# Adjacency network, eight graphs on one core: twenty-four step tiles ahead of the second widening, three guard products in front of the second aggregation, the older normalisation beside the first one

## What is computed

```
x = layernorm(x + attention(x, adj))       # softmax(q k^T * scale, masked by adj) v
x = layernorm(x + leaky(norm_adj @ x @ W.T + b))
x = layernorm(x + heads(x, adj))           # 4 heads: softmax over i of leaky(s_i + s_j), masked; times Wh
x = layernorm(x + (D^-1/2 (adj + I) D^-1/2) @ x @ B)
```

## Time and profile before

| what | us |
|---|---|
| median of 3 runs (lowest to highest) | 1005.48 (1004.79 to 1006.26) |
| the profiled execution | 1003.88 |
| its span, first to last instruction | 1002.0 |
| busy in the span: PE, DVE, ACT, POOL | 860.9, 744.5, 588.7, 334.8 |
| idle of DVE ahead of head minima (L825, both buffers), for ACT's step tiles | 77.2 |
| idle of DVE ahead of layer 3's output, for PE | 37.4 |
| mean granted clock of TensorE | 0.937 of full speed |

### The profile page before, as it was taken

How to read it: one execution, slowest core, us unless ns; L and a number is a source line. 1 busy time by engine, 2 the same in 40 slices (tenths; PEclk the granted TensorE clock), 3 DMA queues, 4 the chain that set the end, 5 groups by cost and what they waited for, 6 DMA issues and landing times.

```text
span 1002.0 us, 25308 instructions
## 1 busy us (share of the span) xinstructions
PE 860.9 (86%) x10852; PEld 689.5 (69%) x10852; DVE 744.5 (74%) x1635; ACT 588.7 (59%) x667; POOL 334.8 (33%) x335
## 2 busy tenths in 40 slices
PE   4985899879999799888998799987998979985774
PEld 3663589747887479855797468964788747973773
DVE  4325775968778695977959788695959779597986
ACT  1672485566764578465764667655685557735432
POOL 2021250416324152243504253240622425134504
PEclk9997899979999999998999999997999999998788
DMA  9701415450356414480174503554044721505100
GB/s 186 114 22 31 97 53 97 86 127 1 85 87 133 80 43 94 66 166 18 43 128 86 128 1 85 87 120 92 17 100 61 165 42 43 106 3 127 43 25 21
DMA packets 166607, 77.91 MB, mean 78 GB/s; under 512 B 136640, under 2 KB 154176, under 8 KB 166496
## 3 DMA queue, kind: packets, MB, share of 16 engines
q1 hardware_dynamic: 157008, 59.00, 28.7%
q0 software_dynamic: 8448, 16.78, 9.4%
q10 hardware_dynamic: 1040, 0.52, 0.2%
HBM read 55.18 MB, written 4.33 MB: 59 GB/s over the span
## 4 chain that ended last, share of the span: by engine, by line
PE 62%; DVE 25%; issue 5%; ACT 4%; POOL 0%; DVEq 0%; POOLq 0%; ACTq 0%
PE ring L1267 12%; PE Z L1282 11%; PE ring L1213 10%; PE ring L1248 9%; PE Z L1235 8%; DVE cmat L825 6%; DVE x L861 3%; PE ring L1211 2%; DVE ring L770 2%; DVE rest L944 2%; PE ring L1176 2%; ACT maskb L608 2%; PE ring L1181 1%; DVE meanvar L854 1%; DVE small L912 1%
## 5 line engine op out<-in xcount | busy, mean ns | idle before, releaser
L660 ACT ACTIVATE steps<-sjrow,steepsi 128x1024 bf16<-128x1024 f32 x248 | 267.3, 1139 | 96.1 <-DVE cmat L825 85.8
L1267 PE MATMUL ring<-vparts,cmat 128*128 128x66 bf16 x4416 | 161.2, 200 | 44.2 <-DVE cmat L825 28.3
L1267 PEld LDWEIGHTS ring<-vparts,cmat 128*128 128x128 f16 x4416 | 154.8, 102 | 50.8 <-DVE cmat L825 32.5
L825 DVE TENSOR_TENSOR cmat<-steps,adj 128x1024 f16<-128x1024 bf16 x180 | 152.0, 893 | 13.0 <-ACT steps L660 11.0
L1213 PE MATMUL ring<-qT,xT 128*128 128x512 f32 x256 | 151.7, 677 | 0.0
L488 POOL TENSOR_SCALAR vareps<-meanvar 128x4 f32<-128x4 f32 x64 | 16.6, 260 | 391.0 <-DVE meanvar L854 391.0
L1235 PEld LDWEIGHTS Z<-vv,probs 128*128 128x128 f32 x1024 | 123.0, 192 | 35.1 <-issue 21.7
L624 ACT ACTIVATE wide<-adjT 128x1024 fp32r<-128x1024 f16 x128 | 124.7, 1045 | 37.5 <-PE Z L1282 37.5
L1235 PE MATMUL Z<-vv,probs 128*128 128x129 f32 x1024 | 125.5, 276 | 13.1 <-ACT probs L667 9.0
L1282 PE MATMUL Z<-wide,parts 128*128 128x512 f32 x512 | 128.1, 402 | 9.6 <-DVE parts L870 5.1
L667 ACT ACTIVATE probs<-ring 128x1024 f32<-128x1024 f32 x64 | 65.3, 1020 | 118.7 <-PE ring L1213 118.7
(11 more groups left out here) (118 smaller groups left out, 1217.4 us busy)
## 6 DMA issues: line engine op xcount, KB each, us to landing
adj<-in_adj_dram POOLq DMA_DIRECT2D x16, 1024.0 KB, 12.8
sjrow<-sj_rows SPq DMA_DIRECT2D x32, 512.0 KB, 4.2
out_dram<-x SPq DMA_DIRECT2D x16, 256.0 KB, 2.4
x<-in_x_dram SPq DMA_DIRECT2D x7, 512.0 KB, 5.5
adjT<-adj SPq DMA_TRANSPOSE x128, 3.4
x<-in_x_dram ACTq DMA_DIRECT2D x1, 512.0 KB, 4.2
small<-in_a_dram SPq DMA_DIRECT2D x1, 128.0 KB, 10.3
sj_rows<-steps SPq DMA_DIRECT2D x8, 16.0 KB
```

Source lines behind the costliest of these rows:

```text
L660: act.activation(steps[:, n % STEPS, :], sjrow[:, h % 2, :], ACT.Relu, bias=steepsi[:, t, h:h + 1], scale=STEEP).then_inc(step_made, 1)
L825: dve.tensor_tensor(c_of[:, t, :], steps[:, n % STEPS, :], adjs[o.parity][:, t, :], ALU.min)\
L1267: last = pe.matmul(s[:, jt, 0:VW], c_of[:, t, jt * P:(jt + 1) * P], vparts[:, t, h, part, :], start=t == 0 and part == 0, stop=t == T - 1 ...
```

## The change

Five orders are changed; no instruction is added or taken out. (1) ACT makes 24 instead of 20 step tiles ahead of the second half of the first widening. (2) In a full step, the guard products 0 to 2 of the following graph run on PE ahead of `agg3` and product 3 between the two outputs of `agg3` (before: only product 0, there; 1 to 3 at the start of the next step). With them, ACT makes mask tiles 0, 1, 2 right after it has taken `xT`, `q` and `v`, and tile 3 after `agg3`; and DVE casts x and q and reads `wh` ahead of `split_x3`, and makes guards 0 to 3 ahead of layer 3's outputs. (3) The statistics and the application of the older graph's last normalisation move on DVE from the context loop to the first aggregation; POOL's 1/sqrt for it and SP's store follow. (4) Head 2's minima are made in one go, and head 3's directly after head 0's combination, ahead of layer 1's outputs; the mask sums are read after head 2's minima. (5) `groups_of` follows the new order of products.

```diff
@@ groups_of
-        if n < 2:
-            seq += of(n, ("s", 0))
-        seq += of(n, *[("s", t) for t in range(1, 5)])
+        seq += of(n, *[("s", t) for t in range(0 if n < 2 else 4, 5)])
...
-        seq += of(n - 1, ("out3", 0))
-        if n > 0:
-            seq += of(n + 1, ("s", 0))
-        return seq + of(n - 1, ("out3", 1))
+        early = n > 0
+        seq += of(n + 1, *[("s", t) for t in range(3) if early]) + of(n - 1, ("out3", 0))
+        return seq + of(n + 1, *[("s", t) for t in (3,) if early]) + of(n - 1, ("out3", 1))
@@ SP step
                     for h in (2, 3):
-                        if kind == "full" and h == 2 and o.base > 0:
-                            store(o.before())
                         fetch_sj(kind, o, h)
...
                         turn_older(kind, o)
+                    if kind == "full" and o.base > 0:
+                        store(o.before())
                     spread_sj(g)
@@ POOL: out of split_values, into step
-                    if kind == "full" and n == 1 and (o.base > 0):
-                        rstd_of(3, o.before())
...
                     degree_of(g)
+                    if kind == "full" and o.base > 0:
+                        rstd_of(3, o.before())
                     for k in range(2):
                         rstd_of(1, g, [k])
@@ ACT step
-                        made = steps_until(20)
+                        made = steps_until(24)
...
+                    masks = kind == "full" and following.base < NB
                     for name, graph, k in (("x2T", g, 0), ("xT", following, 0), ("wh", g, 0), ("wh", g, 1),
                                            ("q", following, 0), ("sj", g, 0), ("v", following, 0)):
...
+                        if masks and name in ("xT", "q", "v"):
+                            make_maskb(following, [("xT", "q", "v").index(name)])
...
-                    make_maskb(Graph(g.base + 1), range(0, 4))
+                    make_maskb(Graph(g.base + 1), range(3, 4))
@@ DVE step
-                guards(kind, g, range(0, 4))
                 if kind == "first":
+                    guards(kind, g, range(0, 4))
...
                 else:
+                    if g.base == 1:
+                        guards(kind, g, range(0, 4))
                     guards(kind, g, range(4, 5))
...
-                    if finish:
-                        norm_stats(3, older, x_of(older), 0)
-                        norm_stats(3, older, x_of(older), 1)
                     guards(kind, g, range(7, T))
...
-                    if finish:
-                        norm_apply(3, older, x_of(older), 0)
-                        norm_apply(3, older, x_of(older), 1)
...
                     mins(kind, o, 1, range(4, T))
-                    sums_of_masks(kind, o, 0)
                 norm_apply(0, g, x_of(g), 1)
                 split_x1(g, 1)
                 if kind == "full":
-                    mins(kind, o, 2, range(0, 4))
+                    mins(kind, o, 2)
+                    if finish:
+                        norm_stats(3, older, x_of(older), 0)
+                        norm_stats(3, older, x_of(older), 1)
+                    sums_of_masks(kind, o, 0)
                     sums_of_masks(kind, o, 1)
-                    mins(kind, o, 2, range(4, T))
+                    if finish:
+                        norm_apply(3, older, x_of(older), 0)
+                        norm_apply(3, older, x_of(older), 1)
                     combine(kind, o, 0)
+                    mins(kind, o, 3)
                 for k in range(2):
                     layer1_out(kind, g, k)
                     norm_stats(1, g, x_of(g), k)
                 if kind == "full":
-                    mins(kind, o, 3, range(0, 4))
                     combine(kind, o, 1)
-                    mins(kind, o, 3, range(4, T))
                 norm_apply(1, g, x_of(g), 0)
                 norm_apply(1, g, x_of(g), 1)
                 if kind == "full":
                     combine(kind, o, 2)
                     end_of_heads(kind, o)
+                largest_si(g)
+                following = Graph(g.base + 1)
+                if following.base < NB:
+                    cast_x(following)
+                    cast_q(following)
+                if kind == "full":
                     split_x3(o, 0)
                     split_x3(o, 1)
-                largest_si(g)
-                if g.base < NB - 1:
-                    cast_x(Graph(g.base + 1))
-                    cast_q(Graph(g.base + 1))
-                if kind == "full":
+                    if following.base < NB:
+                        guards(kind, following, range(0, 3))
+                        guards(kind, following, range(3, 4))
                     layer3_out(kind, o, 0)
                     layer3_out(kind, o, 1)
@@ PE layer3 and step
+                if g.base < NB - 1:
+                    for t in range(3):
+                        guard_scores(kind, Graph(g.base + 1), t)
                 pe.wait_ge(split3, o.count(6, 3))
...
                 aggregate(o, "agg3", parts3, (split3, o.count(6, 6)))
                 if g.base < NB - 1:
-                    guard_scores(kind, Graph(g.base + 1), 0)
+                    guard_scores(kind, Graph(g.base + 1), 3)
...
-                    if g.base < 2:
-                        guard_scores(kind, g, 0)
-                    for t in range(1, 5):
+                    for t in range(0 if g.base < 2 else 4, 5):
                         guard_scores(kind, g, t)
```

More of the change, by code:

```diff
@@ L712, in step @@
                         if graph.base < NB:
-                            take_group(kind, graph if name != "sj" else g, name, k)
+                            take_group(kind, graph, name, k)
+                        if masks and name in ("xT", "q", "v"):
+                            make_maskb(following, [("xT", "q", "v").index(name)])
                 if kind != "first":
```

## The result

| what | before | changed |
|---|---|---|
| median us (lowest to highest) | 1005.87 (1004.79 to 1006.55) | 994.51 (990.97 to 995.89) |
| the profiled execution, its span | 1003.88, 1002.0 | 995.6, 993.8 |
| mean granted clock in it | 0.937 | 0.939 |

The ratio is 0.9883 (0.9853 to 0.9912): 11.4 us less by the medians, where the forecast was 17.3 less (988.2). The span is 8.2 shorter: the six intervals from A to A give 13.8, the part ahead of step 1's A takes back 2.6 and the part behind step 7's A 2.9.

What follows compares the result with a forecast made beforehand. Chain mostly on PE, a quarter on DVE; 56.7 + 6.9 + 49.1 = 112.7 per interval, 114.4 with one low stretch, against 117.7. Over six -19.8, outside +2.5: 1003.9 becomes 986.6, median 988.2; range 974 to 1006.

Steps and rivals of the forecast that it cites:

- Head 0 to the projections: From A (PE ends first aggregation, starts head 0's product): 2.39 saved returns as 4 us wait, `wh` at A+33.6; gain 0.
- ACT between the projections: Mask 0 waits for the adjacency load issued near A+25.7, starts at A+34.1, hidden with 0.7 to spare.
- a sign of being wrong: ACT idle ahead of its first mask, released by the adjacency load.
- Guards: Third aggregation at A+42.8, scores at A+56.7 instead of A+59.2: gain 2.5 (1 to 4) per interval.
- Scores to context, the low stretches: Scores to context products: 6.9 at full clock, before 8.6; per interval none, one or two low stretches, 1.7 each; one taken.
- the case of two: Both PE standstills, at the projections and ahead of the scores, cost a low stretch: 116.1 per interval, 998 us; chance 0.22.
- Context to the next A: Context products to next A: 49.5, less 1.5 of wait, plus 1.1 for the later second widening: 49.1.
- The sum: Interval 112.7, 114.4 or 116.1 with no, one or two low stretches, against 117.7; outside the six intervals +2.5.
- Clock stays up: No low stretch behind PE's standstills at the projections and ahead of the scores: 978 us; chance 0.18.
- Clock falls twice: Low clock behind both standstills, at the projections and ahead of the scores: 998 us; chance 0.22.
- The late matrix: Mask 0 waits for its matrix, delaying `wh`'s evacuation: 4.0 per interval, 1012 us; chance 0.24 (0.09 no change, 0.15 slower).
- It moves and gains nothing: Head 3's reordering only moves PE's wait; already in the forecast at 0, without a chance of its own.

Runs made afterwards that it cites:

- experiment 2: Changed kernel with head 3's minima back in two halves behind layer 1's outputs, as in the kernel before: 988.98 us, ratio 0.9835.
- experiment 9: Changed kernel with extra unread products filling PE's wait ahead of `wh`, and mask 0 behind the second evacuation of `wh`: 987.41 us, ratio 0.9808.
- experiment 3: Changed kernel with 20 step tiles instead of 24 ahead of the second widening and head 2's minima in halves: 991.17 us, ratio 0.9859.
- experiment 6: Changed kernel with head 3's minima back, 20 step tiles, head 2's minima in halves, and 11 unread products ahead of guard product 4: 970.47 us, ratio 0.9650.
- experiment 1: Changed kernel with 14 extra unread products filling PE's wait ahead of `wh`: 987.73 us, ratio 0.9822.
- 4: Changed kernel with guards, mask tiles, casts and largest s_i back where they were before: 1009.55 us, ratio 1.0036.
- 7: Changed kernel with the older normalisation back in the context loop: 1008.69 us, ratio 1.0025.
- 5: Changed kernel with head 3's minima back behind layer 1, 20 step tiles and head 2's minima in halves: 979.51 us, ratio 0.9742.
- 8: Kernel before with the early guards alone (guard products 0 to 3, masks, casts, DVE's guards): 993.32 us, ratio 0.9881.

## Why the prediction was right where it was, and where it failed

**Head 0 to the projections.** Right as a time, wrong as a price. `wh` starts at A+33.3 (forecast 33.6), the wait ahead of it is 3.74 ("about 4"), head 2's is 1.80 (1.7). But "gain 0" counted arrival only. The clock behind the standstill belongs to the price of a wait, and experiment 2 puts it at 5.5 us.

**ACT between the projections.** Right, in part by luck: mask 0 starts at A+34.0 (34.1), but the load is issued at A+24.7 (25.7) and its first half lands 9.1 later (8.4), so two errors cancel. The half issued first landed first in every interval, 8.2 to 9.1 after its issue. The wait is covered (experiment 9), and the third aggregation starts at A+42.3 (42.8) where the clock stood. That ACT stands idle ahead of its first mask was listed as a sign of being wrong; it showed and cost nothing. It was a poor sign: by the forecast's own times ACT has nothing to do there, between the projections that PE reaches near A+29.6 and the landing at A+34.1.

**Guards.** Right: where `wh` kept the clock the scores start at A+56.8 (56.7), with 2.99 of standstill ahead of guard product 4 ("some 3"). Some 0.4 of it is already the low clock, in that product (1.03 at 566.55 against 0.60 at 336.46). DVE's 3.37 were to go; 2.37 are left.

**Scores to context, the low stretches.** The step that failed is the term "I take one, at 1.7". Measured behind A+32 are 3.4 on the mean, two stretches in four of six intervals, and the one at the scores is 3.1 in one. The rows at hand were a standstill of 1.99 without a fall and one of 3.57 with one, and both come from one short interval. In the three long intervals of the same trace the clock fell behind the 1.99 as well, and 3.5 were lost there instead of 1.7 (kernel before, A = 395.10, timeline of PE, then a window):

```profile
448.74 2.22 PE L1161 MATMUL ring<-qxb 128*128 128x512 bf16 x6 [1.99 <-DVE smax L770]
...
450.00:450.50 0.50, 0.50 (x2) 0.50 1.03 209
```

The fall behind the 2.39 in head 3 lay in the same trace too and was not read. Both would have put 3 and 4 us clearly on the side of the falls, and the case of two (998) ahead.

**Context to the next A.** Right: 48.8 in all intervals (49.1), the price of the widening 1.05 by experiment 3 (1.1), the 1.51 gone.

**The sum.** Without any low stretch the terms gave 112.7, and 112.0 was measured (the intervals less their loss; experiment 6, which loses nothing there but has other step tiles, has 110.9 to 112.1). So the other terms came out 0.7 better and the clock 1.7 worse, 1.0 per interval, 6.0 in six. Outside the intervals the forecast was 2.5 and the trace has 5.5. Step 1's A is 2.6 later (1.1): some 1.6 of it is there by the context products of that step, since step 0's transposes start at 85.94 instead of 84.13, ahead of any full step. Neither the change nor an experiment reorders step 0, and in the experiments' profiles these transposes start anywhere from 83.69 to 86.48, so this part belongs to the execution and not to the change. The tail is 2.9 longer (1.4): in step 7 DVE's head sums end 1.2 later and its splitting now stands behind the read of `wh`, the third aggregation starts 2.4 later, and 1.7 of that is left at the last aggregation, which itself takes 9.85 instead of 8.60. 6.0 + 3.0 = 9.0 is the gap between the forecast sum of 986.6 and the profiled 995.6.

**The rivals.** *Clock stays up* holds in two intervals of six at `wh` and in none at the scores; experiment 1 keeps the clock at `wh` alone, and experiment 6 at both places, but with other step tiles and minima. *Clock falls twice* is what mostly happened; its 998 was too high by the 0.7 per interval above, less the 3.0 outside. *The late matrix* was half true, ACT waits, and it costs nothing. *It moves and gains nothing* turned out for head 3 as a loss.

## What to carry to other kernels

A wait that a reordering moves is not worth zero when its end stays the same: what PE runs behind it may run at half the clock, so put a standstill where another engine sets the next arrival anyway, or fill it with products that nobody reads. Before you count low-clock stretches, look at the windows behind every standstill of the kernel before, the covered ones too, and in more than one interval. And when several reorderings come together, time them apart: here two of them held all of the gain, and the other two took more than half of it back.

## What was not expected of the hardware

The same standstill of 3.74 ahead of the same products was followed by 0.50 of granted clock in three intervals of the changed kernel (1.7 to 3.0 us of PE's work lost) and by 1.00 in two; in the sixth, where it was only 2.25 long, it fell too (1.7 lost). Counted over the full-step intervals of all these profiles, the two are the exception:

| standstill of PE | profiles | intervals in which the clock fell behind it |
|---|---|---|
| 3.74, ahead of `wh` | changed, 3, 4, 7 | 21 of 23 |
| 3.57, ahead of the scores, where the clock was not low already | before, 4 | 7 of 7 |
| 2.98, ahead of guard product 4 | changed, 1, 2, 3, 5, 7, 8, 9 | 48 of 48 |
| 2.39, in head 3 (three waits of 0.33 follow) | before, 2, 5, 6, 8 | 30 of 30 |
| 1.99, behind the guards | before, 4 | 5 of 12 |
| 1.80, ahead of head 2 | changed, 1, 3, 4, 7, 9 | 1 of 36 |
| 1.50, ahead of the last context product | before, 7, 8 | 0 of 18 |

So in this kernel the longer standstills were nearly always followed by the low clock and the shorter ones seldom, but the length alone does not decide it. The Trainium skill, "TensorE: Matmul & The Clock Gate", section "What's actually happening", says that the gate's observation runs freely, not aligned with the kernel; that the same 3.74 fell three times and held twice agrees, but no run here shifted the kernel against it. Executions of the changed kernel differ in the clock as in the time: 990.97 at a mean clock of 0.946 and 995.89 at 0.941, while experiment 1, without that standstill, has 0.951. And 14 or 11 small products without use in a wait were worth 6.8 and 9.0 us.
